# The first four raw tiles of a Mamba scan in two halves of 512 tokens, the first halves ahead of the second

## The chip, the cores and the metric

The program runs on one core of one Trainium2 chip and is a single launch. The metric is the device time of the launch in microseconds (us), lower is better. The kernel before was timed in three runs: 2753.62, 2757.24 and 2768.87 us, median 2757.24.

## The reference, cut to what matters

Four blocks stand one after another, each an attention-like part and a feed-forward part added to `x`, after a layer norm. The change is in the third block's attention-like part, a Mamba scan over `x` of shape (2, 1024, 256): batches b = 0 and 1, 1024 tokens each.

```python
zxbcdt = (hidden_states @ W_in + b_in) * mup_vector      # 4640 channels
z, xBC, dt = ...                                         # 2048, 2560, 32 channels
conv = lax.conv_general_dilated(xBC_t, conv_w[:, None, :], (1,), [(K - 1, 0)], ...,
                                feature_group_count=CONV_DIM)      # K = 4, causal, per channel
xBC = silu(conv + conv_b)
x, Bm, Cm = ...                                          # 32 heads x 64, 8 groups x 32, 8 x 32
dt = softplus(dt + dt_bias);  a = exp(dt * -exp(A_log))
states = associative_scan(combine, (a, dt * x * B))      # state = a * state + dt * x * B
y = einsum('blhps,blhs->blhp', states, C) + D * x
y = group_rms_norm(y * silu(z)) * norm_w
return y @ W_out + b_out
```

## The kernel before, in words

Five engines run their own instruction lists: PE (matmul), ACT, DVE, POOL and SP (issues DMAs). They meet by semaphores. The launch is a row of stages; the Mamba scan (class `MambaScan`) stands between two barriers at which all engines wait for each other. The stage ahead of it ends with matmuls of L2265 and two additions of L2324.

A **raw tile** is 128 of the 2560 `xBC` channels times the 1024 tokens of one batch. Tiles 0 to 15 are `x`, 16 and 17 are `B`, 18 and 19 are `C`. Each goes through this chain:

- `raw` on PE (L1780): projection in two parts of 512 tokens, into one of two PSUM banks each (ring A).
- `raw` on ACT (L1916): scale and bias, PSUM into the buffer `RAW` in SBUF. There are two such buffers, used in turn, with three zero columns ahead of the tokens. From the third tile on ACT waits until the taps of the tile two before are done.
- `raw` on POOL (L2085): the convolution's tap 0, 1024 wide, from `RAW` into the tile's place in `BC` or `XC`.
- taps 1, 2 and 3 on DVE (L1990): `out = RAW[k:k+1024] * w_k + out`, each waits for the one before.
- `silu` on ACT (L1923), in place, 1024 wide.

The scan itself is a loop of 32 steps n: batch, group of 4 heads (g), half of the tokens (c4 = 0 or 1). A step has on PE `scan` (L1794), `xd` (transposes of x, L1803), `cb` (C times B, L1819), `cp` (L1808), `st` (chunk states, L1842), `gate` (L1826), `within` (L1862), `across` (L1880), `var` (L1887) and `out` (L1897); on DVE `scan` (L1997), `xd` (L2004), `bd` (L2025), `cb` (L2032), `cp` (L2016, L2018), `h` (state updates, L2041 and L2045) and `end` (L2054). `bt` (L1787 on PE, L1929 on ACT) transposes B once for a group of steps, in two parts of 512 tokens. `sel` on POOL (L2093, L2095) makes the selection matrices that `scan` and `cp` multiply with.

**What sets the order.** A table `AT` gives each kind of work a time of its own, in steps, relative to its n. Each engine sorts its work by these times and does it strictly in that order; a wait at the head holds all that is behind it. PSUM banks are given out when the list is made: ring A (2 banks) to `raw`, `gate`, `var`, `out`, and ring B (3 banks) to `scan`, `bt`, `xd`, `cb`, `cp`, round robin in PE's order. So a PE step waits until the engine that reads its bank's previous user is done with it (`take`).

The first four raw tiles are 16 (B), 0 (x), 18 (C) and 1 (x). Step n = 0 needs tokens 0 to 511 of them, step n = 1 the others.

Of the kernel before, what the change touches and what calls it, by code (L numbers as in the profile page):

```python
# [15 lines left out]
D = 256  # L16
# [3 lines left out]
X0, XNT0, CONST0, WA0, WF0, WK0, EX0, END = 0, 4096, 8192, 9216, 22224, 28672, 52000, 53200  # L20
# [65 lines left out]
class Net:  # L86
# [1542 lines left out]
class MambaScan(Stage):  # L1629
# [26 lines left out]
    def __init__(self, net, mem, norm, clear):  # L1656
# [28 lines left out]
        self.crep = [net.flag("m_crep%d" % i, 64 * 16) for i in range(2)]  # L1685
        self.blank = net.flag("m_blank", 1)

    A, B, S, Y = (0, 1), (2, 3, 4), 7, (5, 6)

    def order(self, engine):  # L1690
# [74 lines left out]
    def pe(self, e, w):  # L1765
# [3 lines left out]
        for step in self.orders["pe"]:  # L1769
# [12 lines left out]
            elif kind == "bt":  # L1782
                _, q, r = step
                p = self.take(w, step, self.B)
                w.wait_ge(self.activations, self.an["silu", q // 2, 16 + q % 2])
                for c in range(4):
# [10 lines left out]
            elif kind == "xd":  # L1797
                p = self.take(w, step, self.B)
                w.wait_ge(self.activations, self.an["silu", b, 2 * g])
                w.wait_ge(self.activations, self.an["silu", b, 2 * g + 1])  # L1800
                for i in range(4):
# [9 lines left out]
            elif kind == "cb":  # L1811
                q = slice(32 * (g % 4), 32 * (g % 4) + 32)
                p = self.take(w, step, self.B)
                w.wait_ge(self.activations, self.an["silu", b, 16 + g // 4])
                w.wait_ge(self.activations, self.an["silu", b, 18 + g // 4])
                for i in range(4):
# [88 lines left out]
    def act(self, e, w):  # L1905
        net, m, A = self.net, self.m, self.activations
        for step in self.orders["act"]:
            kind, n = step[:2]
            if kind == "raw":
# [6 lines left out]
                e.activation(m.RAW[:, r % 2, 3 + tt * 512:3 + tt * 512 + 512], self.bank(step, self.A),  # L1916
                             ACT.Identity, scale=m.mup[:, tile:tile + 1],
                             bias=m.bm[:, tile:tile + 1]).then_inc(A.sem, 1)
            elif kind == "silu":
                _, b, i = step  # L1920
                dst = self.taps(b, i)
                w.wait_ge(self.results, self.dn["tap", b, i, 3])
                e.activation(dst, dst, ACT.Silu, bias=m.cb[:, i:i + 1]).then_inc(A.sem, 1)  # L1923
# [21 lines left out]
            elif kind == "square":  # L1945
                s = step[2]
                c4 = n % 2
                w.wait_ge(self.pooled, self.gn["gate", n, s])
                if n > 0:
                    w.wait_ge(self.products, self.pn["var", n - 1])  # L1950
                    w.wait_ge(self.pooled, self.gn["square", n - 1])
# [23 lines left out]
    def dve(self, e, w):  # L1975
        net, m, D = self.net, self.m, self.results
        S = net.PS[:, self.S, :].rearrange("p (c d) -> p c d", c=8)
        for step in self.orders["dve"]:
# [4 lines left out]
            if kind == "tap":  # L1983
                _, b, i, k = step
                dst = self.taps(b, i)
                if k == 1:
                    w.wait_ge(self.pooled, self.gn["raw", b, i])
                else:
                    w.wait_ge(D, self.dn["tap", b, i, k - 1])
                e.scalar_tensor_tensor(dst, m.RAW[:, self.raw[b, i] % 2, k:k + 1024], m.cw[:, i * 4 + k:i * 4 + k + 1],  # L1990
                                       dst, ALU.mult, ALU.add).then_inc(D.sem, 1)
# [74 lines left out]
    def pool(self, e, w):  # L2066
        net, m, G = self.net, self.m, self.pooled
        e.memset(m.RAW[:, :, 0:3], 0.0).then_inc(self.blank.sem, 1)
        for step in self.orders["pool"]:
            kind, n = step[:2]  # L2070
            if kind == "raw":
                _, b, i = step
                w.wait_ge(self.blank, 1)
                w.wait_ge(self.activations, self.an["raw", b, i, 0])
                w.wait_ge(self.activations, self.an["raw", b, i, 1])
                if i > 15:
# [8 lines left out]
                e.tensor_scalar(self.taps(b, i), m.RAW[:, self.raw[b, i] % 2, 0:1024], m.cw[:, i * 4:i * 4 + 1], 1.0,  # L2085
                                ALU.mult, ALU.mult).then_inc(G.sem, 1)
# [40 lines left out]
    def sp(self, e, w):  # L2127
        m = self.m
        for n in range(self.N):
            b, g, c4 = self.where(n)  # L2130
            half = slice(c4 * 512, c4 * 512 + 512)
            q = slice(32 * (g % 4), 32 * (g % 4) + 32)
            w.wait_ge(self.activations, self.an["silu", b, 18 + g // 4])
            if n > 1:
# [1066 lines left out]
```

## Time and profile before

| | |
|---|---|
| runs | 2753.62, 2757.24, 2768.87 us |
| profiled execution | 2758.55 us, its span from first to last instruction 2756.8 us |
| PE busy | 2609.5 us, 95% |
| DVE, ACT, POOL busy | 1600.0, 1064.4, 925.3 us |
| first `raw` matmul of the Mamba scan | 1809.61 us into the span |
| first state update `h` on DVE | 1851.71 us |
| mean granted TensorE clock | 0.975 of full speed |

Times in the profile count from the span's start. A busy PE is an upper bound, since its instructions are pipelined. "Idle before, releaser" tells how long an engine had stood still ahead of an instruction and whose signal let it go. PEclk is the clock that TensorE was granted: 1.00 is 2.4 GHz and 0.50 is 1.2 GHz.

### The profile page before, as it was taken

The numbers are of one execution on the slowest core, as the hardware profiler recorded it, in microseconds if no ns is written. First come the engines' busy times: TensorE is split into PE (matmuls) and PEld (weight loads), VectorE is DVE, ScalarE is ACT, GpSimd is POOL, SyncE is SP. The second block draws the span as 40 slices with busy tenths as digits, with TensorE's granted clock in tenths as the row PEclk, the third lists the DMA queues.
The fourth block names the chain that finished last, engine by engine and source line by source line (L and its number), as shares of the span: only waits on it lengthen the run. The fifth ranks groups of instructions, "written<-read, shape, count | busy, mean of one in ns | idle before, by whom it ended". The sixth has DMA issues, their size and how long they took to land.

```text
span 2756.8 us, 42000 instructions
## 1 busy us (share of the span) xinstructions
PE 2609.5 (95%) x16786; PEld 1650.9 (60%) x16786; DVE 1600.0 (58%) x3476; ACT 1064.4 (39%) x1954; POOL 925.3 (34%) x934
## 2 busy tenths in 40 slices
PE   7998988999999999999999998879999999979996
PEld 4445444664556565565565556646666666756996
DVE  6675672227575664756655232767778877744332
ACT  2534543114444544445345111534444444433222
POOL 3221210003232222322222001626666767644222
PEclk8999999999999999999999999989999999979998
DMA  6222211009000000000000200000000000035123
GB/s 191 63 62 63 62 47 62 0 1 151 1 1 1 1 1 1 1 1 1 1 16 1 106 0 31 1 12 17 17 17 13 17 13 17 14 130 190 62 72 134
DMA packets 57138, 109.54 MB, mean 40 GB/s; under 512 B 13792, under 2 KB 32480, under 8 KB 55792
## 3 DMA queue, kind: packets, MB, share of 16 engines
q1 hardware_dynamic: 53152, 96.47, 12.6%
q0 software_dynamic: 3792, 10.39, 1.0%
q8 instruction: 133, 2.18, 0.3%
q14 instruction: 61, 0.50, 0.1%
HBM read 71.16 MB, written 27.08 MB: 36 GB/s over the span
## 4 chain that ended last, share of the span: by engine, by line
PE 86%; DVE 8%; ACT 2%; issue 1%; DMA 1%; POOL 1%; SPq 1%; POOLq 0%; DVEq 0%; ACTq 0%
PE ps L1256 9%; PE ps L1238 8%; PE ps L1780 5%; PE ps L1247 5%; PE ps L1228 4%; PE ps L378 4%; PE ps L1265 4%; PE ps L360 4%; PE ps L365 4%; PE ps L1897 4%; PE ps L1826 4%; PE ps L2921 3%; PE ps L2945 3%; PE ps L697 2%; PE ps L721 2%; PE ps L737 2%
## 5 line engine op out<-in xcount | busy, mean ns | idle before, releaser
L1256 PE MATMUL ps<-back 128*128 128x512 f32 x576 | 292.0, 596 | 0.3 <-ACT back L1299 0.3
L1299 ACT ACTIVATE back<-ps 128x512 f32<-128x512 f32 x288 | 170.0, 597 | 263.7 <-PE ps L1247 262.1
L1294 ACT ACTIVATE back<-ps,front 128x128 f32<-128x128 f32 (+7 forms) x256 | 189.1, 739 | 71.7 <-DVE front L1345 69.9
L1388 POOL TENSOR_TENSOR back<-back 128x512 f32<-128x512 f32 x72 | 91.5, 1271 | 361.7 <-DVE back L1333 361.5
L1247 PEld LDWEIGHTS ps<-front,back 128*128 128x128 f32 x1152 | 140.6, 141 | 118.3 <-issue 93.8
L1398 POOL TENSOR_SCALAR back<-back,front 128x128 f32<-128x128 f32 (+5 forms) x192 | 143.0, 749 | 190.9 <-DVE front L1364 188.1
L809 ACT ACTIVATE back<-ps 128x1024 f32<-128x1024 f32 (+1 forms) x192 | 151.0, 811 | 132.0 <-PE ps L721 131.5
L1345 DVE TENSOR_REDUCE front<-ps 128x1 f32<-128x128 f32 (+7 forms) x256 | 194.0, 758 | 8.8
L1247 PE MATMUL ps<-front,back 128*128 128x128 f32 x1152 | 170.5, 273 | 3.6 <-DVE back L1370 3.6
L1338 DVE TENSOR_TENSOR ps<-ps,front 128x128 f32<-128x128 f32 x256 | 76.0, 297 | 166.0 <-PE ps L1238 166.0
L697 PE MATMUL ps<-rounded 128*128 128x512 f32 (+3 forms) x384 | 143.5, 419 | 12.2 <-DMA rounded<-kh 4.5
L1228 PE MATMUL ps<-front 128*128 128x512 f32 x320 | 150.3, 593 | 0.0
L1780 PE MATMUL ps<-front 128*128 128x512 f32 x320 | 147.1, 604 | 1.9 <-ACT back L1916 1.0
L857 DVE CUSTOM_DVE_ANT_0 ps<-ps,back 128x128 f32<-128x128 f32 (+3 forms) x256 | 121.0, 512 | 46.4 <-PE ps L697 44.8
L1238 PE MATMUL ps<-front,back 128*128 128x512 f32 (+3 forms) x384 | 144.4, 487 | 3.4 <-POOL back L1388 3.4
L931 POOL TENSOR_SCALAR_AFFINE_SELECT back<-back 128x256 f32<-128x256 f32 x128 | 51.8, 408 | 283.2 <-ACT back L809 282.8
L1238 PE MATMUL ps<-back 128*128 128x512 f32 (+3 forms) x384 | 145.0, 486 | 0.0
L389 ACT ACTIVATE back<-ps 128x512 f32<-128x512 f32 x64 | 38.2, 597 | 256.1 <-PE ps L360 256.0
L320 POOL TENSOR_TENSOR back<-back,front 128x4 f32<-128x4 f32 x8 | 8.1, 1015 | 384.0 <-DVE back L302 384.0
L402 DVE TENSOR_TENSOR back<-back,ps 128x512 f32<-128x512 f32 x64 | 44.0, 687 | 151.7 <-PE ps L365 143.4
L1826 PE MATMUL ps<-front 128*128 128x512 f32 x256 | 127.0, 618 | 0.0
L697 PEld LDWEIGHTS ps<-rounded 128*128 128x128 f32 x384 | 74.0, 202 | 86.9 <-DVE front L857 37.0
(320 smaller groups left out, 5599.1 us busy)
## 6 DMA issues: line engine op xcount, KB each, us to landing
whole<-l_w SPq DMA_DIRECT2D x32, 512.0 KB
front<-back SPq DMA_DIRECT2D x128, 64.0 KB, 2.0
rounded<-qh SPq DMA_DIRECT2D x28, 256.0 KB
rounded<-kh SPq DMA_DIRECT2D x56, 128.0 KB
front<-xg SPq DMA_DIRECT2D x47, 129.0 KB
xg<-front SPq DMA_DIRECT2D x2, 3008.0 KB, 38.2
front<-l_win SPq DMA_DIRECT2D x1, 4640.0 KB, 17.7
front<-l_wgu SPq DMA_DIRECT2D x2, 2048.0 KB, 13.3
```

The source lines that it names most:

```text
L697: t = e.matmul(o[:, 0:n], self.QS[:, s, h, qt], self.KS[:, s, h, 512 * r:512 * r + n], start=True, stop=True)
L809: e.activation(self.PT[j % 2][:, 2 * a:2 * a + 2, c:512], PS[:, 2 * a:2 * a + 2, c:512], ACT.Exp).then_inc(A.sem, 1)
L1228: t = e.matmul(o, W, XNT[:, k, tok], start=(k == 0), stop=(k == 1))
L1238: t = e.matmul(s[:, c:c + m], self.Q[:, h, qt * 128:qt * 128 + 128], self.Kt[G % 2][:, c:c + m], start=True, stop=True)
L1247: t = e.transpose(p[:, h * 128:h * 128 + 128], self.P[n % 2][:, h, j * 128:j * 128 + 128], net.ident)
L1256: e.matmul(PS[:, 7, :], self.V[:, j, G % 4 * 128:G % 4 * 128 + 128], self.turned(("turn", n, j)), start=(j == 0), stop=(j == qt)).then_inc ...
L1294: e.activation(self.P[n % 2][:, h, :nk], s[:, :nk], ACT.Exp, bias=st[:, 0, h:h + 1], scale=1.0, accum_out=st[:, 1, h:h + 1]).then_inc(A.se ...
L1299: e.activation(self.turned(step), self.bank(step), ACT.Copy).then_inc(A.sem, 1)
L1345: e.tensor_reduce(self.st[n % 2][:, 0, h:h + 1], s[:, :nk], AX.X, ALU.max, negate=True).then_inc(D.sem, 1)
L1398: e.tensor_scalar(self.P[n % 2][:, h, :nk], self.P[n % 2][:, h, :nk], self.st[n % 2][:, 3, h:h + 1], 1.0, ALU.mult, ALU.mult).then_inc(S.s ...
L1780: t = e.matmul(p, m.Win[:, k, col:col + 128], XNT[:, k, tok], start=(k == 0), stop=(k == 1))
L1826: t = e.matmul(p, m.Win[:, k, col:col + 128], XNT[:, k, tok], start=(k == 0), stop=(k == 1))
```

## The change

Tiles 16, 0, 18 and 1 of batch 0 are "halved". For them `raw` on POOL, the three taps on DVE and `silu` on ACT are each issued twice, on 512 tokens, and each engine's order puts the four first halves ahead of the four second ones (`HALVES`, `STEP`, `BEGIN`). Two more RAW buffers (`RAW0`, in the space of `sq` and `O`) hold tiles 18 and 1, so that four tiles are held at once; ACT's wait for the taps starts with the fifth tile, which waits for the second half of tile 16. `bt` of the second half moves from time -0.98 to 0.2. Readers of these tiles wait for the half that they read. All else keeps its place in the table.

```diff
+        self.RAW0 = sb(WA0 + 16960, 2, 1032)
...
+        for m, i in enumerate(self.HALVES):
+            for kind, places in self.BEGIN.get(engine, {}).items():
+                for tt in range(2):
+                    t = places[tt] + self.STEP[tt] * m
+                    if kind == "tap":
+                        for k in (1, 2, 3):
+                            add(t, "tap", 0, i, k, tt)
+                    else:
+                        add(t, kind, 0, i, tt)
         for (n, early), b, i, s in self.conv:
             t = n + early
+            if self.halved(b, i):
+                if i == 18 and engine in ("pe", "act"):
+                    for r, x in enumerate((-1, 0.2)):
+                        add(x + (.01 if engine == "act" else 0), "bt", 0, r)
+                continue
...
+    HALVES = (16, 0, 18, 1)
+    STEP = (0.05, 0.1)
+    BEGIN = {"pe": {"raw": (-2.5, -1.09)}, "act": {"raw": (-2.45, -1.9), "silu": (-1.85, 0.0)},
+             "dve": {"tap": (-1.8, -0.2)}, "pool": {"raw": (-2.45, -1.9)}}
...
+    def part(self, kind, b, i, tt, *k):
+        return (kind, b, i, *k, tt) if self.halved(b, i) else (kind, b, i, *k)
+    def buffer(self, r):
+        return self.m.RAW0[:, r % 2, :] if r in (2, 3) else self.m.RAW[:, r % 2, :]
...
-                w.wait_ge(self.activations, self.an["silu", b, 2 * g])
-                w.wait_ge(self.activations, self.an["silu", b, 2 * g + 1])
+                w.wait_ge(self.activations, self.an[self.part("silu", b, 2 * g, c4)])
+                w.wait_ge(self.activations, self.an[self.part("silu", b, 2 * g + 1, c4)])
...
-                if r > 1:
-                    w.wait_ge(self.results, self.dn["tap", *self.raws[r - 2], 3])
+                if r > 3:
+                    w.wait_ge(self.results, self.dn[self.part("tap", *self.raws[r - (4 if r < 6 else 2)], 1, 3)])
...
-                e.scalar_tensor_tensor(dst, m.RAW[:, self.raw[b, i] % 2, k:k + 1024], m.cw[:, i * 4 + k:i * 4 + k + 1],
+                e.scalar_tensor_tensor(dst, self.piece(self.buffer(self.raw[b, i])[:, k:k + 1024], tt), m.cw[:, i * 4 + k:i * 4 + k + 1],
```

On PE, at the start of the Mamba scan, the kernel before has all eight projections (L1780) first, and both parts of `bt` (L1787) together:

```order
L1780 MATMUL ps<-front 128x512 x16
L1794 MATMUL ps<-rounded 128x256 x2
L1787 MATMUL ps<-front,back 128x128 x8
L1794 MATMUL ps<-rounded 128x256 x2
L1803 MATMUL ps<-front 128x128 x4
L1819 MATMUL ps<-back 64x64 x8
```

In the changed kernel the same place reads as follows (L1817 is `raw`, L1831 `scan`, L1824 `bt`, L1840 `xd`, L1856 `cb`):

```order
L1817 MATMUL ps<-front 128x512 x8
L1831 MATMUL ps<-rounded 128x256 x2
L1817 MATMUL ps<-front 128x512 x2
L1824 MATMUL ps<-front,back 128x128 x4
L1817 MATMUL ps<-front 128x512 x4
L1831 MATMUL ps<-rounded 128x256 x2
L1817 MATMUL ps<-front 128x512 x2
L1840 MATMUL ps<-front 128x128 x4
L1856 MATMUL ps<-back 64x64 x8
```

`scan` of step 0 now stands behind four projections, with the other four behind it; the second part of `bt` has left this place.

It comes back on PE in the middle of step 0, between `scan` of step 1 (L1831) and the second `st` (L1879), ahead of `within`, `xd` and `cb` of step 1 (L1899, L1840, L1856), whose ring B banks it moves on by one:

```order
L1863 MATMUL ps<-front 128x512 x2
L1831 MATMUL ps<-rounded 128x256 x2
L1824 MATMUL ps<-front,back 128x128 x4
L1879 MATMUL ps<-back 32x64 x16
L1899 MATMUL ps<-back 64x64 x16
L1840 MATMUL ps<-front 128x128 x4
L1856 MATMUL ps<-back 64x64 x8
```

On DVE, between `cp` of step 0 (L2016, L2018) and the first `h` (L2041), the kernel before has `scan` of step 1 and the taps of the fifth tile:

```order
L2016 COPY back<-ps 128x8
L2018 TENSOR_TENSOR back<-front,ps 128x512
L1997 SCALAR_TENSOR_TENSOR back<-ps,back 128x512
L1990 SCALAR_TENSOR_TENSOR back<-back,front 128x1024 x3
L2041 COPY back<-ps 128x64
```

In the changed kernel (L2031 taps, L2038 `scan`, L2082 the first `h`) the twelve taps of the second halves stand there too:

```order
L2057 COPY back<-ps 128x8
L2059 TENSOR_TENSOR back<-front,ps 128x512
L2031 SCALAR_TENSOR_TENSOR back<-back,front 128x512 x3
L2031 SCALAR_TENSOR_TENSOR front<-back,front 128x512 x3
L2031 SCALAR_TENSOR_TENSOR back<-front,back 128x512 x3
L2038 SCALAR_TENSOR_TENSOR back<-ps,back 128x512
L2031 SCALAR_TENSOR_TENSOR front<-front 128x512 x3
L2031 SCALAR_TENSOR_TENSOR back<-back,front 128x1024 x3
L2082 COPY back<-ps 128x64
```

They have moved from ahead of `scan` of step 0 to behind its `cp`. On POOL, `sel` stands behind the four first `raw` halves; before, it stood behind the first two whole tiles:

```order
L2085 TENSOR_SCALAR back<-back,front 128x1024
L2085 TENSOR_SCALAR front<-back,front 128x1024
L2093 COPY rounded<-rounded 128x512
L2095 COPY rounded<-rounded 128x256
```

Changed (L2128 `raw`, L2137 and L2139 `sel`):

```order
L2128 TENSOR_SCALAR back<-back,front 128x512
L2128 TENSOR_SCALAR front<-back,front 128x512
L2128 TENSOR_SCALAR back<-front 128x512
L2128 TENSOR_SCALAR front<-front 128x512
L2137 COPY rounded<-rounded 128x512
L2139 COPY rounded<-rounded 128x256
```

Two more tiles' worth of `raw` are issued ahead of `sel`, each half as wide.

## Rows read from the trace of the kernel before

**Rows 1.** The page: what each engine was busy.
```profile
PE 2609.5 (95%) x16786; PEld 1650.9 (60%) x16786; DVE 1600.0 (58%) x3476; ACT 1064.4 (39%) x1954; POOL 925.3 (34%) x934
```

**Rows 2.** Stretches: length, busy PE, PEld, DVE, ACT, POOL, PEclk, DMA, GB/s.
```profile
1809.60:1820.00 10.40, 10.39 (x24) 4.48 (x24) 4.36 (x3) 3.11 (x4) 3.50 (x4) 1.00 0.01 2
1820.00:1830.00 10.00, 4.88 (x15) 2.58 (x15) 8.26 (x7) 6.15 (x7) 5.22 (x4) 0.96 0.00 0
1830.00:1843.00 13.00, 8.91 (x38) 5.57 (x37) 9.29 (x10) 4.39 (x7) 1.43 (x1) 0.51 0.17 41
1843.00:1870.00 27.00, 25.05 (x401) 15.29 (x400) 24.41 (x38) 9.53 (x15) 9.40 (x8) 1.00 0.09 21
1870.00:2420.00 550.00, 547.35 (x7606) 361.74 (x7605) 425.08 (x638) 236.14 (x407) 373.30 (x274) 1.00 0.06 15
```

**Rows 3.** The chain of waits, 1839 to 1870: start, us, what.
```profile
1839.04 5.39 PE ps L1780 x8
...
1844.90 3.43 PE ps L1780 x8
...
1853.52 1.20 DVE back L1990
1854.71 1.13 DVE back L1997
...
1858.04 0.68 DVE back L2004
...
1865.84 1.91 PE ps L1826 x4
...
1868.37 0.59 PE ps L1803 x4
```

**Rows 4.** The timeline, ACT, POOL and DVE: start, us, engine, line.
```profile
1814.33 1.13 POOL L2085 TENSOR_SCALAR back<-back,front 128x1024 f32<-128x1024 f32 x1 [4.61 <-ACT back L1916]
...
1816.78 0.78 ACT L1916 ACTIVATE back<-ps,front 128x512 f32<-128x512 f32 x1 [0.94 <-PE ps L1780]
...
1819.11 1.59 POOL L2093 CAST rounded<-rounded 128x512 fp32r<-128x512 f32 x1
...
1820.65 1.39 POOL L2095 CAST rounded<-rounded 128x256 fp32r<-128x256 f32 x1
...
1822.02 2.09 POOL L2085 TENSOR_SCALAR back<-back,front 128x1024 f32<-128x1024 f32 x1
...
1844.78 0.68 DVE L2018 TENSOR_TENSOR back<-front,ps 128x512 f32<-128x512 f32 x1
...
1846.57 4.99 DVE L1990 SCALAR_TENSOR_TENSOR back<-back,front 128x1024 f32<-128x1024 f32 x3
...
1851.71 0.22 DVE L2041 COPY back<-ps 128x64 f32<-128x64 f32 x1
```

**Rows 5.** Groups by line and shape, 1809.5 to 2430: count, busy us, mean ns.
```profile
L2045 DVE SCALAR_TENSOR_TENSOR back<-back,ps 128x64 f32<-128x64 f32 x224 | 62.3, 278 | 27.5 <-PE ps L1842 21.8
L1952 ACT ACTIVATE front<-back 128x512 f32<-128x512 f32 x64 | 38.4, 627 | 34.4 <-POOL back L2107 34.4
L2054 DVE SCALAR_TENSOR_TENSOR back<-front,ps 128x512 f32<-128x512 f32 x32 | 22.4, 743 | 16.0 <-PE ps L1880 16.0
L1923 ACT ACT_TABLE_LOAD x1 | 1.3, 1283 | 0.0
```

**Rows 6.** The timeline, PE alone: start, us, line.
```profile
1829.23 1.97 PE L1787 MATMUL ps<-front,back 128*128 128x128 f32 x8 [4.14 <-ACT back L1923]
...
1852.78 0.68 PE L1819 MATMUL ps<-back 32*64 32x64 f32 x16
...
1859.38 0.65 PE L1842 MATMUL ps<-back 64*32 64x64 f32 x32 [0.51 <-DVE back L2025]
...
1865.15 0.68 PE L1819 MATMUL ps<-back 32*64 32x64 f32 x16 [0.43 <-DVE back L1997]
```

**Rows 7.** One microsecond, PE alone: length, busy, granted clock, DMA, GB/s.
```profile
1829.00:1830.00 1.00, 0.77 (x4) 0.59 0.00 0
```

More of the change, by code:

```diff
@@ L1745, in wait_read, with piece @@
             w.wait_ge(self.products, self.pn["gate", self.N - 1, s])
+    @staticmethod
+    def piece(x, tt):
+        return x[:, 512 * tt[0]:512 * tt[0] + 512] if tt else x
     def taps(self, b, i):
@@ L1784, in pe @@
                 p = self.take(w, step, self.B)
-                w.wait_ge(self.activations, self.an["silu", q // 2, 16 + q % 2])
+                w.wait_ge(self.activations, self.an[self.part("silu", q // 2, 16 + q % 2, r)])
                 for c in range(4):
@@ L1813, in pe @@
                 p = self.take(w, step, self.B)
-                w.wait_ge(self.activations, self.an["silu", b, 16 + g // 4])
-                w.wait_ge(self.activations, self.an["silu", b, 18 + g // 4])
+                w.wait_ge(self.activations, self.an[self.part("silu", b, 16 + g // 4, c4)])
+                w.wait_ge(self.activations, self.an[self.part("silu", b, 18 + g // 4, c4)])
                 for i in range(4):
@@ L1919, in act @@
             elif kind == "silu":
-                _, b, i = step
-                dst = self.taps(b, i)
-                w.wait_ge(self.results, self.dn["tap", b, i, 3])
+                b, i = step[1:3]
+                dst = self.piece(self.taps(b, i), step[3:])
+                w.wait_ge(self.results, self.dn[("tap", b, i, 3, *step[3:])])
                 e.activation(dst, dst, ACT.Silu, bias=m.cb[:, i:i + 1]).then_inc(A.sem, 1)
@@ L1948, in act @@
                 w.wait_ge(self.pooled, self.gn["gate", n, s])
+                if n == 0:
+                    for r in (2, 3):
+                        w.wait_ge(self.results, self.dn[self.part("tap", *self.raws[r], 1, 3)])
                 if n > 0:
@@ L1983, in dve @@
             if kind == "tap":
-                _, b, i, k = step
-                dst = self.taps(b, i)
+                b, i, k = step[1:4]
+                tt = step[4:]
+                dst = self.piece(self.taps(b, i), tt)
                 if k == 1:
-                    w.wait_ge(self.pooled, self.gn["raw", b, i])
+                    w.wait_ge(self.pooled, self.gn[("raw", b, i, *tt)])
                 else:
-                    w.wait_ge(D, self.dn["tap", b, i, k - 1])
-                e.scalar_tensor_tensor(dst, m.RAW[:, self.raw[b, i] % 2, k:k + 1024], m.cw[:, i * 4 + k:i * 4 + k + 1],
+                    w.wait_ge(D, self.dn[("tap", b, i, k - 1, *tt)])
+                e.scalar_tensor_tensor(dst, self.piece(self.buffer(self.raw[b, i])[:, k:k + 1024], tt), m.cw[:, i * 4 + k:i * 4 + k + 1],
                                        dst, ALU.mult, ALU.add).then_inc(D.sem, 1)
@@ L2071, in pool @@
             if kind == "raw":
[L2072 to L2075, printed above, removed]
+                b, i = step[1:3]
+                tt = step[3:]
+                w.wait_ge(self.blank, 2)
+                for part in tt or (0, 1):
+                    w.wait_ge(self.activations, self.an["raw", b, i, part])
                 if i > 15:
@@ L2084, in pool @@
                         w.wait_ge(self.results, self.dn["end", 2 * before + 1, i % 2])
-                e.tensor_scalar(self.taps(b, i), m.RAW[:, self.raw[b, i] % 2, 0:1024], m.cw[:, i * 4:i * 4 + 1], 1.0,
+                e.tensor_scalar(self.piece(self.taps(b, i), tt),
+                                self.piece(self.buffer(self.raw[b, i])[:, 0:1024], tt), m.cw[:, i * 4:i * 4 + 1], 1.0,
                                 ALU.mult, ALU.mult).then_inc(G.sem, 1)
@@ L2132, in sp @@
             q = slice(32 * (g % 4), 32 * (g % 4) + 32)
-            w.wait_ge(self.activations, self.an["silu", b, 18 + g // 4])
+            w.wait_ge(self.activations, self.an[self.part("silu", b, 18 + g // 4, c4)])
             if n > 1:
```

7 lines of the change are left out of this document (5 added, 2 removed).

## The prediction

> **What bounds the kernel now.** I read the page first. PE is busy for 95% of the span [rows 1], so time is lost or won mainly where PE stands still, or runs at the lower clock. Next, busy time by stretch [rows 2]: from 1870 to 2420 us PE is busy for 547.35 of 550 us while DVE has 425.08. There the scan's loop is bound by PE, and whatever PE is late by at 1870 is handed on to the end, because the order and PE's work after it are the same. Ahead of 1870 PE is busy for 10.39 + 4.88 + 8.91 + 25.05 = 49.2 of 60.4 us, idle for 11.2 us, and between 1830 and 1843 its granted clock is 0.51. That is the start-up that the change rearranges. Third, the chain of waits: up to 1835 it lies mostly on DVE, in the taps (8.26 busy of the 10 us from 1820, PE 4.88 [rows 2]); then on PE, whose fifth raw tile takes 5.39 us for eight matmul records, mostly at the low clock, and whose sixth takes 3.43 us at full clock; then on DVE again, in the `h`, a tap and `scan` [rows 3]. The timeline of PE [rows 6] has the waits: 4.14 us of idleness ahead of `bt` at 1829.23, and it is in that microsecond that the granted clock falls to 0.59 [rows 7]. It stays at that level almost up to 1843 [rows 2].
>
> Marks to compare with: DVE ends `cp` of step 0 at 1844.78 + 0.68 = 1845.46 [rows 4]; first `h` 1851.71 [rows 4]; `cb` of step 1 on PE 1852.78, `st` of step 1 1859.38, `cb` of step 2 1865.15 [rows 6].
>
> **Durations of the halves.** A part of a projection is four records: 3.43 / 2 = 1.71 us [rows 3]. ACT's `raw` is 512 wide already: 0.78 [rows 4]. POOL's tap 0 takes 1.13 for 1024 [rows 4]; half of it is 0.57, I take 0.6. A DVE tap takes 1.20 behind other work [rows 3]. No 512-wide tap from SBUF is in the trace. The nearest rows are the same operation 512 wide from PSUM, 0.743, and 64 wide, 0.278 [rows 5]; below, half of 1.20 is 0.60. I take 0.75, and 0.03 for the wait between taps of one half, 0.78 in all; the ends are 0.60 and 0.80. A half `silu` I take at 0.63, from ACT's 512-wide square [rows 5].
>
> The Trainium skill bears on that size: "VectorE: DVE Perf Modes", section "The TRN2 errata", has a fixed cost per instruction, so that small tiles pay it each time, and gives (N + 151) / 0.96 for a two-tensor fp32 operation. By that page, as an estimate, a half tap is 0.69 us, and the twelve are 0.7 us cheaper than mine; the rule speaks against halving, and the 0.278 us for 64 elements [rows 5] agrees with a fixed part.
>
> **Up to `cp` of step 0: 5.5 us earlier.** Nothing changes at the start, 1809.61. PE does the four first parts without a pause and ends at 1816.5; ACT has the fourth at 1816.78 + 0.78 = 1817.56, as before for its fourth part [rows 4]. DVE's first tap starts at about 1813.4 instead of 1814.33 + 1.13 = 1815.5 [rows 4]: not a bound yet. POOL ends its fourth half `raw` at 1817.56 + 0.2 + 0.6 = 1818.4 and only then does `sel`, 1.59 + 1.39 = 3.0 us [rows 4], to 1821.4. `scan` of step 0 waits for it on PE, and behind `scan` the other four projections are queued: 4.6 us of idleness that is new. Then, on PE unless named (where no row is given the step is small, and an estimate from its neighbours): `scan` 0.4 and part 1 of tile 16, 1.71, to 1823.5; ACT 0.78, table load 1.28 [rows 5], half `silu` 0.63, to 1826.3; half of `bt` 0.8 (both took 1.97, [rows 6]), to 1827.1; two parts 3.43, to 1830.5; `scan` 0.4; the last part 1.71, to 1832.6; ACT 0.78 and the copy of `bt` 0.6, to 1834.1, which frees the bank of `cb`; `cb` 0.68 [rows 6]; `xd` 0.6; the fifth tile at full clock 3.43; `cp` 0.3, to 1839.1. DVE follows with 0.2 + 0.68: 1840.0, against 1845.46. DVE's first halves cost 12 x 0.78 = 9.4 us, and about 2.8 us beside POOL's `raw` and `sel`, from 1813.4 to 1825.6. They are hidden, since DVE waits for PE's second `scan` at 1830.9 anyway.
>
> **From there to the first `h`: 9.4 us more work.** The twelve second-half taps no longer stand ahead of `cp` but behind it: 9.4 us. The rest, `scan` of step 1 and the fifth tile's taps, took 1851.71 - 1845.46 = 6.25 us, with three taps at 4.99 instead of 3.7 because POOL worked beside them [rows 4]. First `h`: 1840.0 + 9.4 + 6.25 = 1855.7, 4.0 us later than before. PE cannot use the time ahead: its sixth tile waits for ACT, which may overwrite tile 16's buffer only after its second-half taps, at about 1842.3, and `xd` of step 1 waits for `silu` of tile 1's second half.
>
> What POOL does to a tap shows in its `raw` of 2.09 us instead of 1.13, beside taps [rows 4]. The Trainium skill, "SBUF — State Buffer", section "Who interferes with whom", says that a DVE instruction with two SBUF inputs and a GpSimd instruction that reads SBUF exclude one another for their whole length. By that rule the 1.3 us of blocking stays in the 6.25; if the halves let POOL in between, it would go and the sum be 1.3 less.
>
> **To the steady loop: 5.6 us late.** The second half of `bt` now takes a ring B bank in the middle, and each later step there gets the next one. `cb` of step 1 thereby waits for DVE's second `scan` of step 1, where before it waited for the first, done by 1846.57, when the taps behind it started [rows 4]. DVE reaches that `scan` after six `h` (1853.52 - 1851.71 = 1.8), a tap (1.20) and itself (1.13) [rows 3, 4]: 1855.7 + 4.1 = 1859.8, against 1852.78 for `cb` before. Behind `cb` on PE are queued `gate`, `within`, `xd`, `across`, `cp` and `st`. So `xd` of step 1 ends at 1859.8 + 0.68 + 1.91 + 0.6 + 0.59 = 1863.6 (`cb`, `gate`, `within`, `xd`; [rows 3, 6]); DVE's matching step started at 1858.04 before [rows 3], so it is 5.6 us late, and what follows on DVE (`bd`, `cb`, tap, `end`, `cp`, `scan`) hands this to `cb` of step 2: 1865.15 + 5.6 = 1870.7. PE's own work (`across` to `xd` of step 2, the small steps some 4.5 us and a `gate` of 1.91) would bring it there at 1870.0. At full clock the change costs 5.6 us.
>
> **The clock.** Ahead of that `cb` PE is idle for some 6 us (1853 to 1859.8). In the trace there was a fall at the end of 4.14 us of idleness [rows 6, 7]. With a fall, `gate` takes twice its 1.71 us: 1.7 us more. Bounds: 0, and 3.4 if the small steps behind it suffer as well. I take 1.7. That the fall of 1829 goes is in the sum already (3.43 for the fifth tile).
>
> Sum: +5.6 + 1.7 = +7.3 us on the profiled execution's 2758.55, 2765.9. The median of the runs, 2757.24, is 1.3 lower; on it I forecast 2764.5. Twelve taps, four tap-0 and four `silu` more are else hidden under PE after 1870.
>
> **Rivals.**
> - Cheap halves. Half taps at 0.60 and no fall of the clock: 12 x 0.18 = 2.2 less behind `cp`, 5.6 - 2.2 = +3.4, 2760.6. For it: throughput dominates the 1.20; against it: 0.743 for the nearest 512-wide row [rows 5].
> - Cold front. The new idleness at 1816.8 to 1821.4 is as long as the one after which the clock fell. The four second projections then run at 1.2 GHz; each is 1.7 us longer, two of them hidden beside ACT's table load: +3.4 to +6.8. Time 2769.5. Against it: the old fall came only in the last microsecond of its gap, behind work with idle spots, and here the work ahead is dense.
> - The front's gain survives (faster). One mechanism: `cp` of step 0 comes early enough to pay for the taps put behind it. `sel` and `bt` would have to cost PE nothing, so that `cp` ends by 1836.5, with half taps at 0.60 (7.2 us) and POOL's 1.3 us of blocking gone: first `h` at 1836.5 + 7.2 + 4.95 = 1848.7, `cb` of step 1 4.1 later, at 1852.8 as before, and PE's idleness after 1843, 27.0 - 25.05 = 2.0 us [rows 2], is filled: 2757.24 - 2.0, 2755. It decides at `cp`: if it ends after 1838, the change cannot be faster. For it: the chain began on DVE, and PE was busy for only 4.88 of the 10 us from 1820 [rows 2]. Against it: `sel` alone is 3.0 us [rows 4].
>
> **How the numbers follow.** Forecast 0.50 (own range 2761 to 2768), cheap halves 0.20, cold front 0.18, faster 0.12. Range: 2752 to 2775, from the rival on the other side, less the spread of the runs, up to cold front at its upper price. A measurement of this kernel can tell some 0.5% (13.8 us) from no change. The whole idleness ahead of 1870 is 11.2 us, so a gain of 13.8 is next to impossible: faster 0.02. Slower by 13.8 needs both falls of the clock at their full price: 0.07. The same: 0.91.
>
> **What would show it.** In the changed profile: PE idle ahead of the first `scan` for 4 to 5 us, with `sel` as its releaser; `cp` of step 0 on DVE ending near 1840; half taps of 0.7 to 0.8 us; first `h` near 1855.7; PE idle for about 6 us ahead of `cb` of step 1, released by DVE's `scan`, and a granted clock near 0.5 behind it; PE busy throughout from 1872. I am wrong if `cb` of step 1 starts ahead of 1856, if half taps take under 0.65, or if the lag at `cb` of step 2 does not reach the end.

## The result, and the profile after

The changed kernel took 2766.28 us (median of 7 runs, 2764.97 to 2767.78) against 2757.24 of the kernel before (7 runs, 2753.62 to 2768.87): +9.0 us, ratio 1.0033 with a 95% interval of 1.0021 to 1.0045. The forecast was 2764.5, range 2752 to 2775, "the same" at 0.91: the loss is a third of a per cent, under the prediction's 0.5%, but the interval leaves out 1.0: it is there. The profiled execution took 2767.78 us (span 2766.0).

The busy times moved little: in the page of the profile after, VectorE (DVE) has 2.7 us and 12 instructions more than before [rows 1], PE the same 16786.

```profile
PE 2609.8 (94%) x16786; PEld 1651.0 (60%) x16786; DVE 1602.7 (58%) x3488; ACT 1064.1 (38%) x1958; POOL 924.1 (33%) x939
```

Stretches of the profile after, columns as in [rows 2]. The scan's first matmul is at 1811.52 us here, 1.9 later than before; that comes from stages ahead of the change, so I count from that matmul from here on.

```profile
1809.60:1820.00 10.40, 8.16 (x24) 3.65 (x22) 5.18 (x7) 3.11 (x4) 3.73 (x6) 1.00 0.01 2
1820.00:1830.00 10.00, 4.98 (x12) 2.42 (x13) 6.62 (x8) 3.39 (x4) 2.75 (x4) 0.67 0.00 0
1830.00:1843.00 13.00, 12.08 (x49) 6.05 (x48) 4.16 (x5) 4.42 (x7) 3.50 (x4) 0.86 0.08 21
1843.00:1880.00 37.00, 26.08 (x390) 14.97 (x389) 32.61 (x48) 12.59 (x18) 9.64 (x8) 0.86 0.09 23
1880.00:2430.00 550.00, 547.41 (x7584) 362.30 (x7582) 425.11 (x637) 235.58 (x407) 372.24 (x273) 1.00 0.06 15
```

The last row is the steady loop, busy for 547.41 of 550 us as before (547.35 [rows 2]): nothing is won back there. The fourth is the new shape: 10.9 us of PE idleness, with DVE busy for 32.61 of 37 us.

The timeline of PE after (start, us, line; in brackets idle time ahead and releaser) has the waits one by one.

```profile
1811.52 7.13 PE L1817 MATMUL ps<-front 128*128 128x512 f32 x16 [0.90 <-DVEq L176]
1822.12 0.50 PE L1831 MATMUL ps<-rounded 128*128 128x256 f32 x2 [3.46 <-POOL rounded L2139]
...
1828.09 1.12 PE L1824 MATMUL ps<-front,back 128*128 128x128 f32 x4 [2.90 <-ACT back L1960]
1828.99 5.89 PE L1817 MATMUL ps<-front 128*128 128x512 f32 x8
...
1847.09 5.40 PE L1817 MATMUL ps<-front 128*128 128x512 f32 x8 [3.72 <-ACT back L1953]
...
1863.85 1.12 PE L1856 MATMUL ps<-back 32*64 32x64 f32 x16 [5.58 <-DVE back L2038]
1864.90 3.37 PE L1863 MATMUL ps<-front 128*128 128x512 f32 x4
...
1876.65 0.68 PE L1856 MATMUL ps<-back 32*64 32x64 f32 x16 [0.43 <-DVE back L2038]
```

PE waits for `sel` (L2139 on POOL) ahead of the first `scan`, and for the half `silu` (L1960) ahead of `bt`. The projection at 1847.09 waits 3.72 us for ACT (L1953), which waits for tile 16's second-half taps. `cb` of step 1 (1863.85) waits 5.58 us for DVE's second `scan`. Twice eight projection records take 5.4 to 5.9 us instead of the 3.43 of full clock [rows 3], and `gate` behind `cb` takes 3.37 instead of 1.9. The granted clock (last column but two), one microsecond each, PE alone:

```profile
1823.00:1824.00 1.00, 1.00 (x3) 0.68 0.00 0
1833.00:1834.00 1.00, 1.00 (x3) 0.71 0.00 0
1847.00:1848.00 1.00, 0.91 (x2) 0.62 0.00 0
1850.00:1851.00 1.00, 1.00 (x2) 0.67 0.00 0
1861.00:1862.00 1.00, 0.00 (x0) 0.50 0.52 127
1867.00:1868.00 1.00, 1.00 (x2) 0.64 0.00 0
```

It fell from 2.4 to 1.2 GHz three times (1823 to 1833, 1847 to 1850, 1861 to 1867): behind the new waits of 3.46 and 3.72 us, and inside the one of 5.58. Before, it fell once, at 1829 [rows 7].

DVE's timeline after:

```profile
1843.25 0.68 DVE L2059 TENSOR_TENSOR back<-front,ps 128x512 f32<-128x512 f32 x1
1843.85 2.32 DVE L2031 SCALAR_TENSOR_TENSOR back<-back,front 128x512 f32<-128x512 f32 x3
1846.08 2.32 DVE L2031 SCALAR_TENSOR_TENSOR front<-back,front 128x512 f32<-128x512 f32 x3
1848.32 3.42 DVE L2031 SCALAR_TENSOR_TENSOR back<-front,back 128x512 f32<-128x512 f32 x3
1851.66 1.21 DVE L2038 TENSOR_TENSOR_SCAN back<-ps,back 128x512 f32<-128x512 f32 x1
1852.80 3.12 DVE L2031 SCALAR_TENSOR_TENSOR front<-front 128x512 f32<-128x512 f32 x3
1855.83 3.92 DVE L2031 SCALAR_TENSOR_TENSOR back<-back,front 128x1024 f32<-128x1024 f32 x3
1859.67 0.22 DVE L2082 COPY back<-ps 128x64 f32<-128x64 f32 x1
```

Undisturbed, the groups of three half taps start 2.235 us apart (1843.85, 1846.08, 1848.32), 0.745 for each tap; beside POOL's tap 0 and `sel` one such group took 3.42 us, and beside a tap 0 alone another took 3.12. From the end of `cp` (1843.93) to the first `h` (1859.67) VectorE does not stand still: 15.74 us.

POOL's first `sel` after, in two parts, ahead of which the four half `raw` stand:

```profile
1820.20 1.06 POOL L2137 CAST rounded<-rounded 128x512 fp32r<-128x512 f32 x1
1821.21 0.85 POOL L2139 CAST rounded<-rounded 128x256 fp32r<-128x256 f32 x1
```

### The profile page after: what moved, and what is told of

It is laid out like the page before. It is cut to its first block, busy times and chain, and to the rows that moved or that the text cites. A ratio compares the mean times of both kernels' runs of the same rounds, so it can differ in the third digit from the quotient of the medians.

```text
span 2766.0 us, 42018 instructions
## 1 busy us (share of the span) xinstructions
PE 2609.8 (94%) x16786; PEld 1651.0 (60%) x16786; DVE 1602.7 (58%) x3488; ACT 1064.1 (38%) x1958; POOL 924.1 (33%) x939
## 4 chain that ended last, share of the span: by engine, by line
PE 86%; DVE 8%; ACT 2%; issue 1%; DMA 1%; POOL 1%; SPq 1%; POOLq 0%; DVEq 0%; ACTq 0%
PE ps L1256 9%; PE ps L1238 8%; PE ps L1817 5%; PE ps L1247 5%; PE ps L1228 5%; PE ps L378 4%; PE ps L1265 4%; PE ps L360 4%; PE ps L365 4%; PE ps L1934 4%; PE ps L1863 4%; PE ps L2965 3%; PE ps L2989 3%; PE ps L721 2%; PE ps L697 2%; PE ps L737 2%
## 5 line engine op out<-in xcount | busy, mean ns | idle before, releaser
L1817 PE MATMUL ps<-front 128*128 128x512 f32 x320 | 150.3, 614 | 4.6 <-ACT back L1953 3.7
L1228 PE MATMUL ps<-front 128*128 128x512 f32 x320 | 152.1, 599 | 0.0
L1863 PE MATMUL ps<-front 128*128 128x512 f32 x256 | 128.4, 624 | 0.0
```

The costliest lines, as they stand in the source:

```text
L1228: t = e.matmul(o, W, XNT[:, k, tok], start=(k == 0), stop=(k == 1))
L1817: t = e.matmul(p, m.Win[:, k, col:col + 128], XNT[:, k, tok], start=(k == 0), stop=(k == 1))
L1863: t = e.matmul(p, m.Win[:, k, col:col + 128], XNT[:, k, tok], start=(k == 0), stop=(k == 1))
```

## The experiments

All marks are from one profiled execution of each kernel, in us behind the scan's first matmul: DVE's end of `cp` of step 0, DVE's first `h`, PE's `cb` of step 2, PE's projection of the seventh raw tile (the start of the steady loop, as the chain of waits has it). The time is the median of 5 to 12 runs. The ratio is against the kernel before, run beside it on the same chip (its medians there: 2755.25 to 2757.24); it is not the quotient of the two medians, and differs from it by up to some 0.1%. The kernels are explained below, in the order of the questions that they answer.

| kernel | `cp` 0 | first `h` | `cb` 2 | 7th raw | time | ratio [95%] |
|---|---|---|---|---|---|---|
| before | 35.85 | 42.10 | 55.54 | 60.14 | 2757.24 | |
| changed | 32.41 | 48.15 | 65.13 | 69.72 | 2766.28 | 1.0033 [1.0021, 1.0045] |
| buffers only | 34.92 | 41.16 | 54.62 | 59.21 | 2757.86 | 0.9997 [0.9987, 1.0006] |
| halves, old order | 35.42 | 41.66 | 55.12 | 59.71 | 2758.08 | 0.9996 [0.9983, 1.0009] |
| `sel` first | 26.63 | 42.41 | 60.32 | 64.91 | 2764.40 | 1.0022 [1.0012, 1.0031] |
| `bt` late | 31.99 | 47.71 | 61.17 | 65.76 | 2762.05 | 1.0017 [1.0008, 1.0026] |
| both | 29.67 | 45.41 | 58.86 | 63.45 | 2757.86 | 0.9995 [0.9987, 1.0004] |
| both, taps behind `h` | 26.76 | 39.90 | 58.37 | 65.20 | 2764.70 | 1.0029 [1.0019, 1.0039] |
| busy front | 32.14 | 47.88 | 64.96 | 69.56 | 2771.21 | 1.0045 [1.0032, 1.0058] |
| busy middle | 32.41 | 48.15 | 63.30 | 67.89 | 2764.76 | 1.0028 [1.0016, 1.0040] |
| taps ahead of `cp` | 41.22 | 47.91 | 64.73 | 69.32 | 2765.81 | 1.0030 [1.0014, 1.0046] |
| fifth tile early | 31.52 | 37.70 | 51.16 | 55.75 | 2753.50 | 0.9975 [0.9961, 0.9989] |
| fifth and sixth early | 32.86 | 38.82 | 52.26 | 58.51 | 2757.16 | 0.9989 [0.9975, 1.0002] |
| halves, fifth early | 32.52 | 38.47 | 51.91 | 58.15 | 2754.61 | 0.9998 [0.9988, 1.0008] |

### The parts of the change by themselves

The kernel before with the four raw buffers: `HALVES = ()` in the changed kernel.

> The kernel before with the four RAW buffers alone: whole tiles of 1024, the old order, no halves. Theory (order): ACT and PE no longer wait at 1820 for the taps, POOL has its tap 0 in time (1.67 us of DVE idleness goes), DVE's taps still end near 1832: 0 to 3 us less than before, 2754 to 2757. It holds nothing of the change's loss. Rival (the buffers in the space of sq and O cost something): 2760 or more.

Measured: 2757.86, no change (0.9997). The marks come 0.9 us earlier, which the time does not show. The buffers are neither a loss nor a gain that can be measured.

Both halves of a tile in a row, tiles in the old order:

```diff
-    STEP = (0.05, 0.1)
-    BEGIN = {"pe": {"raw": (-2.5, -1.09)}, "act": {"raw": (-2.45, -1.9), "silu": (-1.85, 0.0)},
-             "dve": {"tap": (-1.8, -0.2)}, "pool": {"raw": (-2.45, -1.9)}}
+    STEP = (0.09, 0.09)
+    BEGIN = {"pe": {"raw": (-2.5, -2.48)}, "act": {"raw": (-2.45, -2.43), "silu": (-1.4, -1.38)},
+             "dve": {"tap": (-1.8, -1.78)}, "pool": {"raw": (-2.45, -2.43)}}
-                    for r, x in enumerate((-1, 0.2)):
+                    for r, x in enumerate((-1, -0.98)):
```

> The changed kernel with both halves of a tile next to each other on every engine, in the old order of the tiles, and both parts of bt where they were: halves and buffers without the reordering. Theory (order is what costs; a half tap is 0.745 us by the changed kernel's trace, so 24 of them cost 17.9 us against 14.4 for twelve at 1.20): the 3.5 us lie ahead of scan on the old chain, less the gain of the buffers: 2 to 4 us over before, 2759 to 2761, well under the changed kernel's 2766. Rival (size alone explains the loss): 2765 to 2767.

Measured: 2758.08 (0.9996), first `h` 0.4 earlier. The 2 to 4 us of loss that the theory expected are not there either. DVE's busy time between first matmul and first `h` (length, busy), first of the kernel before, then of this one, then of the changed one:

```profile
1809.61:1851.71 42.10, 28.71 (x25) 0.84 0.08 19
```

```profile
1808.61:1850.27 41.66, 32.16 (x36) 0.84 0.08 20
```

```profile
1811.52:1859.67 48.15, 31.43 (x36) 0.86 0.04 11
```

With halves VectorE works 3.4 us more and stands still 3.9 us less (13.39 before, 9.50 here), mostly because its first tap starts two microseconds sooner (3.84 us behind the first matmul instead of 5.96). In the changed order it works 2.7 us more and stands still 3.3 us more: a sum of 6.05. So halving costs no time that can be measured as long as the old order is kept; with the new order the loss appears.

### What holds PE: `sel` and the second part of `bt`

`sel` of step 0 put ahead of POOL's first tap 0:

```diff
-                        add(n + x, kind, n, *([r] if len(places) > 1 else []))
+                        early = -2.7 if kind == "sel" and n == 0 else n + x
+                        add(early, kind, n, *([r] if len(places) > 1 else []))
```

> The changed kernel with sel of step 0 at the head of POOL's list, ahead of the four half raws. Theory (order): the first scan on PE no longer waits for sel (3.46 us in the changed kernel's trace), the granted clock does not fall at 1823, so cp of step 0 comes 5 to 9 us earlier and the time falls by 4 to 8 us, to 2758 to 2762. Rival (size: the halves cost what they cost because each half tap carries a fixed part, 24 at 0.745 instead of 12 at 1.20): sel's place does not matter, under 1 us, 2765 to 2767.

Measured: PE no longer waits ahead of the first `scan` (first line below): `cp` is 5.8 us earlier than in the changed kernel, the seventh tile 4.8. POOL has the two parts of `sel` done in 0.61 and 0.40 us, since DVE is idle there. PE with `sel` first:

```profile
1812.54 0.80 PE L1832 MATMUL ps<-rounded 128*128 128x256 f32 x2
...
1852.57 1.11 PE L1857 MATMUL ps<-back 32*64 32x64 f32 x16 [4.46 <-DVE back L2039]
1853.61 3.78 PE L1864 MATMUL ps<-front 128*128 128x512 f32 x4
```

The wait ahead of `cb` of step 1 (second line) is still there. The clock falls three times here too, only later: at 1817, in the wait of 2.90 us for the half `silu`, at 1834 and at 1851. The eight projection records behind the second fall take 6.55 us, the `gate` behind the third 3.78. The median, 2764.40, is only 1.9 us under the changed kernel's and misses the expected 2758 to 2762; the twelve runs lie between 2757.71 and 2768.20, and the profiled one is the fastest of them.

Second part of `bt` behind `xd` of step 1:

```diff
-                    for r, x in enumerate((-1, 0.2)):
+                    for r, x in enumerate((-1, 1 - 0.6 + 0.05)):
```

> The changed kernel with the second part of bt behind xd of step 1 on PE, so that cb of step 1 gets the ring B bank that DVE's first scan of step 1 frees, as before. Theory (banks): cb, gate and within of step 1 (0.68 + 1.91 + 0.62 us) run inside the 5.58 us wait, xd waits instead: 3 to 5 us less, 2761 to 2763. Rival (DVE alone sets the pace through h): st of step 1 comes no earlier, under 1 us, 2765 to 2767.

Measured: 2762.05, 4.2 us under the changed kernel, as the theory expected. PE with `bt` late: `cb` of step 1 and the `gate` behind it run at once and at full clock; the wait comes later, at `xd`, and is 2.91 us. The seventh tile is 4.0 earlier than in the changed kernel.

```profile
1856.52 0.68 PE L1856 MATMUL ps<-back 32*64 32x64 f32 x16
1857.13 1.99 PE L1863 MATMUL ps<-front 128*128 128x512 f32 x4
...
1862.65 0.85 PE L1840 MATMUL ps<-front 128*128 128x128 f32 x4 [2.91 <-DVE back L2038]
```

Both together:

> The changed kernel with both single moves: sel at the head of POOL's list and the second part of bt behind xd of step 1. Theory: they add, since one acts ahead of cp of step 0 and the other behind it: median of sel first (2764.4) less 4.2, 2758 to 2761; at most 1 us over the same when the clock falls at no bad place. Rival (one wait replaces the other): no better than 2762.05.

Measured: 2757.86 (0.9995), the loss is gone. The seventh tile is 3.3 us behind the kernel before in the profiled execution, but this one, the slowest of the eleven (2768.65), came to the scan at a lower clock, and its first 16 records took 9.98 us instead of 7.13:

```profile
1816.66 9.98 PE L1818 MATMUL ps<-front 128*128 128x512 f32 x16 [0.90 <-DVEq L176]
```

Without those 2.85 us the lag is 0.46, an estimate that `cp` supports (29.67 - 2.85 = 26.82, with `sel` first alone 26.63); 9.6 less 4.8 less 4.0 would be 0.8. So at the marks the two waits are separate costs and add up. In the medians the single moves give 1.9 and 4.2 us and both together 8.4. Taken singly, their intervals overlap that of the changed kernel; that of both together does not. That the two waits make the loss is thus shown by the times, the share of each only by one trace.

### The clock

Four extra matmuls (into a free bank) ahead of the first `scan`, where PE waits for `sel`:

```diff
                 p = self.take(w, step, self.B)
+                if n == 0 and step[2] == 0:
+                    for _ in range(4):
+                        e.matmul(net.PS[:, self.Y[0], :], m.Win[:, 0, 0:128], XNT[:, 0, 0:512], start=True, stop=True)
                 w.wait_ge(self.pooled, self.gn["sel", n // 2 * 2])
```

> The changed kernel with four matmuls of 512 columns more, into a bank that nobody has written yet, ahead of the first scan: 3.4 us of PE work in a wait of 3.46 us, nothing moved. Theory (clock): the granted clock stays at 1.00 from 1823 to 1834, the five projections there take 1.71 us each instead of up to 2.9, and the time falls by 2 to 3.5 us, to 2763 to 2764.5. Rival (that stretch is set by ACT and DVE): under 0.5 us.

Measured, PE with the busy front:

```profile
1820.16 1.88 PE L1817 MATMUL ps<-front 128*128 128x512 f32 x4
1824.94 1.12 PE L1824 MATMUL ps<-front,back 128*128 128x128 f32 x4 [2.90 <-ACT back L1963]
1825.85 6.11 PE L1817 MATMUL ps<-front 128*128 128x512 f32 x8
```

The projection behind `scan` is at full clock (1.88), but then PE waits 2.90 us for `silu`, and the clock falls there: the next eight records take 6.11. `cp` is 0.3 us earlier, and the time is not better: the median of five runs, 2771.21, is 4.9 us above the changed kernel's. My theory that filling this one wait would save the low clock fell: it only moved the fall to the next wait. Why the median is worse stays open, since the profiled execution is the fastest of the five (2765.39).

Six extra matmuls ahead of `cb` of step 1:

```diff
+                if n == 1:
+                    q1 = self.take(w, ("gate", 0, 1), self.A)
+                    for _ in range(6):
+                        e.matmul(q1, m.Win[:, 0, 0:128], XNT[:, 0, 0:512], start=True, stop=True)
```

> The changed kernel with six matmuls of 512 columns more ahead of cb of step 1, into the ring A bank that gate takes next: 5.2 us of PE work in a wait of 5.58 us. Theory (clock): gate of step 0 takes 1.98 us instead of 3.37 and cb 0.68 instead of 1.12, the time falls by 1.5 to 2 us, to 2764.5. Rival (the lag is DVE's by then): no difference over 0.5 us.

Measured, PE with the busy middle:

```profile
1854.07 5.32 PE L1853 MATMUL ps<-front 128*128 128x512 f32 x12
1859.81 0.68 PE L1860 MATMUL ps<-back 32*64 32x64 f32 x16 [0.42 <-DVE back L2042]
1860.42 1.98 PE L1867 MATMUL ps<-front 128*128 128x512 f32 x4
```

`cb` 0.68 and `gate` 1.98 instead of 1.12 and 3.37: 1.83 us, as the marks say (69.72 to 67.89). That is the price of the cold `cb` and `gate`; here no other fall took their place. In the medians it is 2766.28 against 2764.76, with intervals that overlap.

### Where the second halves' taps stand

Ahead of the scan of step 0 instead of behind `cp`:

```diff
-             "dve": {"tap": (-1.8, -0.2)}, "pool": {"raw": (-2.45, -1.9)}}
+             "dve": {"tap": (-1.8, -1.5)}, "pool": {"raw": (-2.45, -1.9)}}
```

> The changed kernel, with the second halves' taps of the first four tiles put on VectorE ahead of the scan of step 0 instead of behind cp of step 0. My theory (12 taps of 0.745, 9 us in a row, are paid wherever they stand on the path from sel to the first h): cp of step 0 comes 6 to 9 us later than in the changed kernel, the first h and cb of step 1 within 2 us of the changed kernel's, and the time is 2764 to 2769. Rival (the loss of the changed kernel is the taps' place behind cp alone): first h 5 us or more earlier than the changed kernel's, time 2757 to 2760.

Measured: `cp` 8.8 later than in the changed kernel, first `h` 0.2 earlier, 2765.81. The 9 us of taps cost the same ahead of `cp` and behind it as far as the first `h` goes, so their place behind `cp` is not the loss by itself. VectorE with the taps ahead waits for the second projections:

```profile
1822.03 2.33 DVE L2031 SCALAR_TENSOR_TENSOR back<-back,front 128x512 f32<-128x512 f32 x3 [1.69 <-POOL back L2128]
1828.44 2.78 DVE L2031 SCALAR_TENSOR_TENSOR front<-back,front 128x512 f32<-128x512 f32 x3 [4.08 <-POOL front L2128]
```

`sel` first, `bt` late, and the fifth and sixth tiles' taps behind the eighth `h`:

```diff
-                    add(t + at["tap%d" % k][s], "tap", b, i, k)
+                    places = {(0, 2): (0.52, 0.52, 0.52), (0, 3): (0.62, 0.62, 0.72)}.get((b, i))
+                    add(places[k - 1] if places else t + at["tap%d" % k][s], "tap", b, i, k)
```

> The former kernel, with DVE's taps of the fifth and sixth tile moved from ahead of the first h to behind the eighth, since only step 2 reads these tiles. Theory (the twelve second-half taps hurt because they stand, with the others, ahead of h): h, across and scan of step 1 come some 4 to 5 us earlier, and the time falls by 2 to 4 us below the former kernel, to 2754 to 2758. Rival (DVE's total work ahead of scan of step 2 sets the lag, in whatever order): no difference from the former kernel, 2758 to 2761.

Measured: 2764.70, 6.8 more than with both moves alone, which neither theory expected. Less the 2.85 us of the low clock there, the first `h` comes 2.7 us earlier (39.90 against 42.56) and the seventh tile 4.6 later. PE then waits one step on:

```profile
1863.11 0.69 PE L1901 MATMUL ps<-back 64*64 64x64 f32 x32 [1.92 <-DVE back L2097]
1866.07 1.09 PE L1842 MATMUL ps<-front,back 128*128 128x128 f32 x4 [2.26 <-ACT back L1962]
```

The `xd` of step 2 needs the fifth and sixth tiles. Put off, their taps are due there. An earlier `h` is worth nothing when the tiles behind it come later.

### A better order

The kernel with buffers only, and the fifth tile's projection (with its copy on ACT) in the wait ahead of `bt`:

```diff
-                    add(t + at["raw"][s], "raw", b, i, *([] if engine == "pool" else [tt]))
+                    at_raw = {("pe", 0, 2): -1.05, ("act", 0, 2): -1.3}.get((engine, b, i), t + at["raw"][s])
+                    add(at_raw, "raw", b, i, *([] if engine == "pool" else [tt]))
```

> The kernel before with four raw buffers, and the fifth tile's raw matmuls and its copy on ScalarE moved ahead of `bt`, where TensorE stood idle for 4.14 us in the kernel before and the 5.39 us of those matmuls later stood between xd and cp of step 0. My theory (what stands between the sel of step 0 and the first h on TensorE is the price of an order, and the size of the tiles is not): cp of step 0 comes 4 to 5 us earlier against the scan's first matmul than in the kernel before, the first h 3 to 5 us earlier, and the time is 2751 to 2754. Rival (the eighth tile's taps, not cp, then set the first h, or the clock falls once more): first h at most 1 us earlier, time 2756 to 2759.

Measured: 2753.50, ratio 0.9975 [0.9961, 0.9989], with `cp` 4.3 and the first `h` 4.4 us earlier than before, and the seventh tile 4.4. It beats both kernels, and the interval leaves out 1.0; the medians are 3.7 us apart (the kernel before took 2757.17 beside it), the ratio says 7 us. PE with the fifth tile early:

```profile
1825.47 3.59 PE L1818 MATMUL ps<-front 128*128 128x512 f32 x8
1828.90 1.04 PE L1825 MATMUL ps<-front,back 128*128 128x128 f32 x8
1836.19 0.79 PE L1832 MATMUL ps<-rounded 128*128 128x256 f32 x2 [6.25 <-DVE back L2039]
...
1863.17 1.98 PE L1864 MATMUL ps<-front 128*128 128x512 f32 x4
```

The tile takes 3.59 us at full clock where PE stood idle for 4.14 [rows 6], instead of 5.39, mostly at the low clock, between `xd` and `cp` [rows 3]. The clock still falls, inside the wait of 6.25 us ahead of the second `scan`; but no raw tile stands between `xd` and `cp` behind it any more. The sixth tile as well, `("pe", 0, 3): -0.9, ("act", 0, 3): -1.15`:

> As the kernel with the fifth tile early, and the sixth tile's raw matmuls and copy moved ahead of cp of step 0 as well. My theory: TensorE has then less to do behind cp, so that the seventh and eighth raw tiles and their taps come earlier; up to 3 us beyond the kernel with the fifth tile early, 2749 to 2753. Rival: TensorE's work only changes its place, since cp of step 0 is then pushed back by as much; the time is that of the kernel with the fifth tile early, within 1 us.

Measured: 2757.16, 3.7 us above the kernel with the fifth tile early; neither theory. PE with both early:

```profile
1838.81 1.11 PE L1841 MATMUL ps<-front 128*128 128x128 f32 x4 [1.37 <-ACT back L1967]
...
1855.15 0.66 PE L1841 MATMUL ps<-front 128*128 128x128 f32 x4 [1.89 <-DVE back L2039]
...
1865.06 3.59 PE L1864 MATMUL ps<-front 128*128 128x512 f32 x4
```

On ACT the sixth tile's copy (1.43 us) now stands ahead of the copy of `bt`, for which `xd` waits 1.37: `cp` is 1.3 late. With less work for PE behind `cp` there is a new gap of 1.89, and a `gate` at the low clock (3.59).

Last, halves in the old order with the fifth tile early:

> The first four tiles in halves, both halves of a tile in a row in the old order of tiles, with the fifth tile's raw matmuls ahead of `bt` (the kernel with the fifth tile early, and halves on top). What stands behind it: between the scan's first matmul and the first h, VectorE was busy 28.71 us in the kernel before and 32.16 with halves in the old order (halves cost about 3.4), and idle 13.39 and 9.50 us (halves start its taps 2 us earlier). My theory (halves buy the earlier start with as much work on VectorE, so they are worth nothing even in the best order): first h 36.5 to 38.5 us behind the scan's first matmul, against 37.70 with the fifth tile early alone; time 2752 to 2756. Rival (with TensorE's wait filled, the earlier start of the taps reaches the end): first h 35 to 36, time 2748 to 2751.

Measured: 2754.61, with the kernel before at 2755.25 beside it (0.9998). VectorE's first tap starts 2.1 us earlier than with whole tiles, yet the first `h` is 0.8 later: with whole tiles, then with halves (length, busy):

```profile
1811.40:1849.10 37.70, 29.33 (x24) 0.86 0.09 22
```

```profile
1809.51:1847.98 38.47, 31.93 (x36) 0.87 0.09 21
```

Halves buy 1.8 us less idleness with 2.6 us more work. A `gate` at the low clock (3.58) makes up the rest of the seventh tile's 2.4. Even in the best order here halves are worth nothing: with them the fifth tile's gain is gone.

## Why the prediction was right

It was right on the sign, the place and nearly on the size; the sum, put against what was measured, all from the first matmul:

| term | forecast | measured |
|---|---|---|
| `cp` of step 0 | 5.5 earlier (30.4) | 3.4 earlier (32.41) |
| `cp` to first `h` | 15.7 | 15.74 |
| first `h` to `cb` of step 1 | 4.1 | 4.18 |
| `cb` of step 1 to `cb` of step 2 | 10.9, and 1.7 for a cold `gate` | 12.80 |
| lag at `cb` of step 2 | +7.3 | +9.6 |
| time | 2764.5 | 2766.28 |

- **The path.** The prediction said that `cp` comes sooner and that the twelve taps then stand behind it in full. They do. A half tap was put at 0.78 with the wait between two of them; undisturbed it took 0.745. But six of the twelve stood beside POOL's work, and the twelve took 10.8 us (1843.85 to 1855.83, less 1.14 for `scan`) instead of 9.4, while the fifth tile's three whole taps were let off and took 3.92 instead of the 4.99 of [rows 4]. That the sum of the two still came out right (15.7 and 15.74) was luck. By the estimate from "VectorE: DVE Perf Modes" of the Trainium skill a half tap was 0.69; undisturbed, dependent ones are 0.745 here, so the measurement decides. The taps beside POOL's reads, 3.42 and 3.12 us instead of 2.32, agree with its "SBUF — State Buffer", section "Who interferes with whom".
- **`sel` and `cb`.** The two waits were named. `sel` held PE for 3.46 us, not 4.6, because its two parts took 1.06 and 0.85 beside half taps, and not 1.59 and 1.39 [rows 4]. `cb` of step 1 waited 5.58 against "some 6". The experiments with `sel` first and with `bt` late each take away one, are worth 4.8 and 4.0 us at the seventh tile of one trace, and together the whole loss in the median. So the pair is shown as the cause, the share of each less firmly.
- **The mis-sized term is the clock ahead of `cp`.** One fall was in the sum, at `gate` (1.7; the busy middle measures 1.83). The forecast had the front at full clock and left its fall to the rival "cold front" at 0.18. It fell, at 1823. Up to the end of `bt` nothing shows of it, 17.5 us both forecast and measured: `sel` was 1.2 us sooner, and the part of tile 16 behind it took 1.0 longer. The two second parts behind `bt` then took 5.3 us instead of 3.43 (1828.99 to 1834.32), and these 1.9 are nearly the 2.0 by which `cp` missed its mark. They are read from one trace; no run took this fall away without opening another. The rival had the mechanism right and the price too high (3.4 to 6.8), since the clock was back at 1833. The argument against it, that the work ahead was dense, was wrong.
- **The fall at 1847** was foreseen by no one and cost nothing: from 1843 to 1863 the chain of waits ran on VectorE alone.
- **From the lag to the time.** The lag of 9.6 us at the seventh tile and the +9.0 of the medians do not match as well as it seems. In the two profiled executions the start of the scan is 1.9 us later and the rest, from the seventh tile to the end, 2.3 us shorter (887.1 and 884.8 us), which makes +9.2. In all fourteen traces that rest lies between 883.7 and 887.1 us, so "is handed on to the end" holds only to some 3 us.
- **Faster** was to be had only with `cp` by 1838; it was at 1842 when counted from before's first matmul (1809.61 + 32.41). With `sel` first, `cp` is 9.2 us earlier than before, and the kernel is still slower, because `bt` and the taps remain: there the condition "`cp` by 1836.5" was met and did not do, since the rival asked for a `bt` without cost too.

Open: how much of the +9.0 is the clock in all. No variant kept it high throughout, and the time of one and the same kernel moves by some us from execution to execution (`sel` first: 2757.71 to 2768.20). The marks stand on one execution of each kernel. The profiled executions also come to the scan at different times (1805.89 to 1816.66), by stages that no variant touches; why is open.

## What to carry to other kernels

When an early start is bought by cutting work in two, ask what happens to the second half: here it was only moved from ahead of one mark to behind it, and the waits that the new order opened (a selection matrix, a bank handed on round robin) cost all of the loss. Such a loss is not seen in the busy times, which hardly moved: look for the new waits, take each away by itself and then both. Look first for an idle gap on the engine that bounds, and for later work on the path that fits into it whole: moving the fifth tile into a gap of 4.14 us gave 3.7 us in the median without splitting anything, though it took four buffers. Count a cold clock behind each new gap that lies on the path, not behind the longest alone.

## What the runs showed of the hardware

- The granted clock fell from 2.4 to 1.2 GHz behind waits of 3.46 and 3.72 us in the changed kernel and in one of 2.90 in the kernel with the busy front. Filling the wait ahead of the first `scan` moved the fall to the next wait; filling the one ahead of `cb` of step 1 took it away without another.
- A dependent tap (two operands in SBUF, fp32) takes 0.745 us at 512 wide, and 1.20 at 1024 wide behind other work [rows 3]: two halves cost a quarter more than a whole. Beside POOL's work three half taps took up to 3.42 us instead of 2.32.
- POOL's `sel` of step 0 took 0.61 + 0.40 us with DVE idle (`sel` first), 1.06 + 0.85 beside half taps, and 1.59 + 1.39 beside whole ones [rows 4].
